# Cross-attention units of four heads by 256 tokens, and one time axis for all steps of the attention plan

## The reference

```python
x = x + attn(layernorm(x))          # 16 heads of 16; blocks of 128 tokens, each sees itself (causal) and the block before
x = x + xattn(layernorm(x), ctx, mask)   # 16 heads of 16; 77 context tokens, mask by token and context position
x = x + ffn(layernorm(x))           # gate/up 256 -> 704, silu(gate) * up, down; 8-bit fake quantisation of x, weights and h
```

## Time and profile before

| | before |
|---|---|
| median of 3 runs | 944.12 us (940.3 to 950.16) |
| the profiled execution | 945.94 us |
| its span, first to last instruction | 944.2 us |
| mean granted clock of TensorE | 0.866 |
| PE / DVE / ACT / POOL busy | 77% / 58% / 44% / 20% of the span |
| setup until the first score unit | 0 to 72 us |
| attention phases | 72 to 788 us |
| last chain to `out`, then the FFN | 788 to 944 us |

### The profile page before, as it was taken

The page is one execution under the profiler, slowest core; times in us unless marked ns, Lnnn a source line. Parts: engine busy times, 40 slices in busy tenths (PEclk is TensorE's granted clock), DMA queues, the critical chain, the costliest instruction groups (busy, mean ns, idle before and its releaser), DMA issues.

```text
span 944.2 us, 13998 instructions
## 1 busy us (share of the span) xinstructions
PE 728.0 (77%) x5008; PEld 412.4 (44%) x5008; DVE 544.3 (58%) x970; ACT 418.8 (44%) x610; POOL 192.4 (20%) x231
## 2 busy tenths in 40 slices
PE   3769888888788997989788778689795684468755
PEld 2446455555545443556445443435343221323344
DVE  4378546665854457566465753345652730559977
ACT  3414544434443544643343455132351342169865
POOL 4002121211321202110231031002002000334536
PEclk9968988899998999999898989688797565679979
DMA  8540141504221344151215413130344012000013
GB/s 258 181 134 3 51 134 42 141 14 115 70 82 30 94 104 109 48 150 48 63 47 134 98 41 86 37 108 14 86 108 130 14 40 45 0 1 1 1 45 134
DMA packets 59187, 71.78 MB, mean 76 GB/s; under 512 B 24635, under 2 KB 36079, under 8 KB 59119
## 3 DMA queue, kind: packets, MB, share of 16 engines
q1 hardware_dynamic: 43792, 50.90, 16.8%
q10 hardware_dynamic: 15327, 19.99, 10.6%
HBM read 17.74 MB, written 4.72 MB: 24 GB/s over the span
## 4 chain that ended last, share of the span: by engine, by line
PE 23%; DVE 12%; issue 6%; DMA 6%; ACT 4%; ACTq 4%; POOL 0%; SPq 0%; POOLq 0%; DVEq 0%
PE banks L676 6%; DMA oc<-sums 4%; PE banks L666 4%; ACTq L906 3%; PE banks L623 2%; PE banks L625 2%; PE banks L549 2%; DVE tops L1280 1%; PE banks L720 1%; PE banks L594 1%; DMA sums<-ls 1%; ACT big L882 1%; PE banks L596 1%; PE banks L653 1%; DVE big L1274 1%
## 5 line engine op out<-in xcount | busy, mean ns | idle before, releaser
L1109 DVE TENSOR_REDUCE mneg<-banks 128x4 f32<-128x1024 f32 (+1 forms) x128 | 145.7, 1152 | 73.8 <-PE banks L587 73.2
L1370 POOL TENSOR_SCALAR_AFFINE_SELECT big<-big 128x512 f32<-128x512 f32 x128 | 85.1, 665 | 448.3 <-ACT big L878 446.9
L878 ACT ACTIVATE big<-banks 128x1024 f32<-128x1024 f32 (+1 forms) x128 | 124.1, 973 | 107.1 <-PE banks L616 74.4
L584 PE MATMUL banks<-big 96*128 96x256 bf16 (+1 forms) x512 | 101.6, 296 | 22.2 <-DVE mneg L1109 9.1
L882 ACT ACTIVATE big<-banks 77x1024 f32<-77x1024 f32 x64 | 64.8, 1019 | 110.7 <-PE banks L625 84.6
L549 PE MATMUL banks<-xnT,weights 128*128 128x512 f32 x192 | 91.7, 607 | 3.0 <-DVE big L1082 1.2
L653 PE MATMUL banks<-big 128*17 128x256 f32 (+1 forms) x1152 | 80.1, 371 | 16.8 <-POOL big L1370 16.7
L1113 DVE TENSOR_REDUCE mneg<-banks 128x8 f32<-128x616 f32 x64 | 49.7, 793 | 68.9 <-PE banks L596 68.7
L616 PE MATMUL banks<-big 99*128 99x256 bf16 (+1 forms) x512 | 76.4, 273 | 9.7 <-ACT big L878 5.6
L587 PE MATMUL banks<-causal,identb 128*128 128x256 bf16 x256 | 77.6, 305 | 0.0
L584 PEld LDWEIGHTS banks<-big 96*128 96x128 bf16 x512 | 51.0, 109 | 58.8 <-issue 28.9
(11 more groups left out here) (150 smaller groups left out, 1165.2 us busy)
## 6 DMA issues: line engine op xcount, KB each, us to landing
big<-parts SPq DMA_DIRECT2D x288, 128.0 KB, 2.5
oc<-sums ACTq DMA_DIRECT2D x16, 512.0 KB
oTs<-oe ACTq DMA_DIRECT2D x64, 64.0 KB, 2.7
out_dram<-oTs SPq DMA_DIRECT2D x16, 256.0 KB, 2.1
xs<-in_x_dram SPq DMA_DIRECT2D x3, 1024.0 KB, 10.1
big<-oe ACTq DMA_DIRECT2D x32, 64.0 KB, 2.9
oTx<-oe ACTq DMA_DIRECT2D x32, 64.0 KB, 2.6
big<-kparts SPq DMA_DIRECT2D x96, 9.6 KB, 2.6
```

Of the source, the lines that this page charges most:

```text
L584: e.matmul(bank(p, j)[:, i * 256 + lo * 128:i * 256 + 256], Q[0:96, hh, c * 128:c * 128 + 128], K[0:96, hh, (c - 1 + lo) * 128:(c + 1) * 1 ...
L878: e.activation(pt[u].rearrange("p (i n) -> p i n", i=4)[:, :, 0:n], pair(p).rearrange("p j (s n) -> p (j s) n", s=2)[:, :, 0:n], ACT.Exp, ...
L1109: e.tensor_reduce(M.rearrange("p (h c) -> p h c", h=4)[:, :, c], pair(p).rearrange("p j (s n) -> p (j s) n", s=2)[:, :, lo * 128:256], AX. ...
L1370: e.affine_select(out=P[:, :, 0:128], in_=P[:, :, 0:128], compare_op=ALU.is_ge, fill=0.0, base=0, pattern=[[0, 4], [1, 128]], channel_mult ...
```

## The change

**Cross units.** Unit j of a cross phase is now tokens 256 j to 256 j + 255 of all four heads. A score unit is two banks (z); each gets two score matmuls of 256 columns and one mask matmul of 512 columns that reads the 256 mask columns twice. A val unit is four matmuls of 256 columns, one in each quarter of the array's columns; the bank of `acc` is still `j // 2`, and its halves are filled in turn.

**One time axis.** `PHASE_US` gives a self phase a length of 20 and a cross phase one of 11. `put` adds each step at `start + t * length`, `start` running over the phases, and all steps of all phases are sorted once and handed to the planner in one go. So a time below 0 or above 1 now reaches into the neighbouring phase. The last two vals of a phase are at 0.01 and 0.065 of the next one, behind its `score` 0 (at 0). The max steps of the next phase run from 0.04 (before -0.3) to 0.62, and those of a self job that follows a cross job from -0.75. `rows` is the last of these. Other times are moved by a few hundredths, the forced `proj` group has a time of its own (0.98), and followers are counted in steps as before.

```diff
--- before.py
+++ after.py
@@ -28,6 +28,7 @@
 AT = {j: n for n, j in enumerate(JOBS)}
 UNITS = {"s": NC, "x": 4}
 HALF_AT = {"s": 3, "x": 1}
+PHASE_US = {"s": 20.0, "x": 11.0}
 
 
 
@@ -157,42 +158,48 @@
     fw = weight_steps()
     fw_at = {28: (0, 1), 29: (1, 9), 30: (9, 15), 31: (15, 20)}
     tail, normed = [], {("s", 0)}
+    timed, start = [], 0.0
+
+    def put(steps):
+        timed.extend(((start + t * length, len(timed) + i, step) for i, (t, step) in enumerate(steps)))
+
     for p in range(2 * len(JOBS)):
         n, g = divmod(p, 2)
         job, units = JOBS[n], UNITS[JOBS[n][0]]
-        steps = [(-1, ("force", "rows"))] + over(-0.5, -0.1, tail)
+        length = PHASE_US[job[0]]
+        put([(-0.001, ("force", "rows"))] + over(0.01, 0.12, tail))
         for j in range(units):
-            steps.append((j / units, ("score", job, g, j)))
+            put([(j / units, ("score", job, g, j))])
             if j > 1:
-                steps.append((j / units + 0.001, ("val", job, g, j - 2, False)))
+                put([(j / units + 0.002, ("val", job, g, j - 2, False))])
         tail = [("val", job, g, units - 2, False), ("val", job, g, units - 1, True)]
         if p + 1 < 2 * len(JOBS):
-            steps += over(-0.3, 0.62, max_steps(p + 1))
+            early = job[0] == "x" and g == 1 and JOBS[n + 1][0] == "s"
+            put(over(-0.75 if early else 0.04, 0.62, max_steps(p + 1)))
         last = JOBS[n - 1] if n else ("s", 0, 0)
         if g == 0:
             if n + 1 < len(JOBS):
-                steps += over(0.05, 0.1, [("bulk", JOBS[n + 1], 1, z) for z in range(2)])
+                put(over(0.13, 0.18, [("bulk", JOBS[n + 1], 1, z) for z in range(2)]))
                 if JOBS[n + 1][0] == "s":
-                    steps += over(0.1, 0.5, [("v", JOBS[n + 1], c0) for c0 in (0, 4)]) if n else []
+                    put(over(0.14, 0.5, [("v", JOBS[n + 1], c0) for c0 in (0, 4)]))
                 else:
-                    steps += [(0.1, ("xkeys", JOBS[n + 1])), (0.15, ("bulk", JOBS[n + 1], 0, 1))]
-            if n == 0:
-                steps += over(0.05, 0.3, [("v", JOBS[1], c0) for c0 in (0, 4)])
+                    put([(0.14, ("xkeys", JOBS[n + 1])), (0.19, ("bulk", JOBS[n + 1], 0, 1))])
             if last[2] == 1 and (job[0] == "s" or last[0] == "x"):
-                steps += over(0.7 if job[0] == "s" else 0.9, 1.0, out_steps(*last[0:2]))
+                put(over(0.7 if job[0] == "s" else 0.85, 0.99, out_steps(*last[0:2])))
             if n + 2 < len(JOBS) and JOBS[n + 2][0:2] not in normed:
-                steps += over(0.0, 0.45, stats_steps(*JOBS[n + 2][0:2]))
+                put(over(0.0, 0.45, stats_steps(*JOBS[n + 2][0:2])))
                 normed.add(JOBS[n + 2][0:2])
         else:
             if last == ("s", last[1], 1) and job[0] == "x":
-                steps += over(0.1, 0.8, out_steps(*last[0:2]))
+                put(over(0.1, 0.8, out_steps(*last[0:2])))
             if n + 2 < len(JOBS):
-                steps += over(0.08, 0.7, [("force", "norm")] + qk_steps(JOBS[n + 2]))
+                put(over(0.1, 0.7, [("force", "norm")] + qk_steps(JOBS[n + 2])) + [(0.98, ("force", "proj"))])
             if last == ("x", last[1], 1):
-                steps += over(0.05, 1.0, third_steps(last[1]))
+                put(over(0.05, 0.97, third_steps(last[1])))
         if p in fw_at:
-            steps += over(0.2, 1.0, fw[slice(*fw_at[p])])
-        o.run([s for _, s in sorted(steps, key=lambda it: it[0])] + ([("force", "proj")] if g else []))
+            put(over(0.2, 0.97, fw[slice(*fw_at[p])]))
+        start += length
+    o.run([s for _, _, s in sorted(timed, key=lambda it: it[0:2])])
     o.run(tail)
     o.run([("force", "acc"), ("force", "weights")])
     a, z = out_steps("x", NB - 1), last_third_steps(NB - 1)
@@ -617,13 +624,14 @@
                                          ks[r][0:99, i, j * 128:j * 128 + 128], qs[r][0:99, i, j * 128:j * 128 + n],
                                          start=(i % 2 == 0), stop=True, skip_group_check=True)
                     else:
-                        blk, two = j // 2, j % 2
-                        for i in range(2):
-                            hh = 2 * two + i
-                            e.matmul(bank(p, i)[0:KX, :], xks[r][0:99, hh, :], qs[r][0:99, hh, blk * 512:blk * 512 + 512],
-                                     start=True, stop=False)
-                            t = e.matmul(bank(p, i)[0:KX, :], identb[0:KX, 0:KX], maskt[0:KX, blk * 512:blk * 512 + 512],
-                                         start=False, stop=True)
+                        keep = maskt[0:KX, j * 256:j * 256 + 256].rearrange("p (a n) -> p a n", a=1)
+                        for z in range(2):
+                            for i in range(2):
+                                e.matmul(bank(p, z)[0:KX, i * 256:i * 256 + 256], xks[r][0:99, 2 * z + i, :],
+                                         qs[r][0:99, 2 * z + i, j * 256:j * 256 + 256], start=(i == 0), stop=False,
+                                         skip_group_check=True)
+                            t = e.matmul(bank(p, z)[0:KX, :].rearrange("p (i n) -> p i n", i=2), identb[0:KX, 0:KX],
+                                         keep.to_broadcast([KX, 2, 256]), start=False, stop=True, skip_group_check=True)
                     t.then_inc(t_score, 1)
                 elif k == "val":
                     _, job, g, j, end = s
@@ -654,17 +662,16 @@
                                              va[f][:, j, 4 * g + i, :], P[:, i, a:z], start=new,
                                              stop=(j == 7 or z - a == 128), tile_position=(0, 32 * i), skip_group_check=True)
                     else:
-                        blk, two = j // 2, j % 2
                         if j == 0 and g == 0:
                             e.wait_ge(d_xv, 2 * n_of["xkeys", job])
                             e.wait_ge(p_one, 2 * n_of["xkeys", job])
                         if j == 2:
                             e.wait_ge(a_evac, before)
                         e.wait_ge(a_exp, n_of["score", job, g, j])
-                        for q in range(2):
-                            i = 2 * two + q
-                            t = e.matmul(acc[:, blk][32 * i:32 * i + 17, :], xv[r][0:KX, i, 0:17],
-                                         pt[u][0:KX, q * 512:q * 512 + 512], start=True, stop=True, tile_position=(0, 32 * i))
+                        for i in range(4):
+                            t = e.matmul(acc[:, j // 2][32 * i:32 * i + 17, (j % 2) * 256:(j % 2) * 256 + 256],
+                                         xv[r][0:KX, i, 0:17], pt[u][0:KX, i * 256:i * 256 + 256], start=(j % 2 == 0),
+                                         stop=True, tile_position=(0, 32 * i), skip_group_check=True)
                     t.then_inc(t_val, 1)
                 elif k == "out":
                     _, kind, b, c = s
```

## The result

| | before | changed |
|---|---|---|
| median, lowest and highest of four runs, us | 944.14 (940.3 to 950.16) | 989.98 (987.35 to 995.17) |
| ratio to before, with its 95% interval | | 1.0486 (1.0416 to 1.0556) |
| span of the profiled execution, us | 944.2 | 989.0 |
| mean granted clock | 0.866 | 0.85 |
| end of the last `val`, us | 787.7 | 833.0 |

The kernel is 45.8 us slower. The forecast was 972 us with a range of 928 to 998. In the kernel after, `max` is L591 and L601, `turnm` L611, `score` L623 and L630, `val` L661 and L672, `out` L683, `scale` L1153, the select L1377, and the DMA of the maxima is issued at L875.

What follows compares the result with a forecast made beforehand. PE's own work was taken to set the pace until 600 us, then chains of waits with PE at half speed. Terms -18 + 9 + 32 - 8 + 8 + 5 = +28 gave 972 us for the median, range 928 to 998.

Steps and rivals of the forecast that it cites:

- term 3: At phase boundaries, score 0 moved ahead of the tail waits for the row maxima to land: +32 us, bounds 0 and +45.
- Term 1: Cross units of four heads by 256: cheaper value matmuls, scores unchanged, -18 us, nearly all on PE's path.
- Term 2: At 31 phase boundaries, more changes between kinds of matmul, two more pieces each at 0.22 us: +9 us.
- Term 4: Max units no longer bunched, so fewer waits for banks VectorE or an exponential still holds: -8 us, bounds 0 and 17.
- Term 5: Chains from the last val to the output projection start later, behind score 0 and a max or two: +8 us.
- Term 6: New waits of 2 to 4 us at boundaries make PE's clock fall, three losses of 1.7 us: +5, bounds 0 and +25.
- The rival that priced fifteen falls at 1.7: The clock falls at nearly every boundary, fifteen new falls instead of three: +20, 992 us; chance 0.14.
- The faster rival: Maxima have landed when PE reaches score 0, so tail waits go and none replace them: -26, 918 us; chance 0.17.
- the draw: Waits for the maxima swallow other waits, +12 instead of +32, and the clock costs nothing: -1, 943 us; chance 0.17.

Runs made afterwards that it cites:

- e1: Kernel before with only the change's new cross units (four heads by 256), in the old order of steps: 938.48 us, ratio 0.9955.
- e10: e1, but from the third job on the maxima's DMA goes to DRAM and score 0 does not wait for it: 932.74 us, ratio 0.9873.
- e9: Changed kernel, but from the third job on the maxima's DMA goes to DRAM and score 0 does not wait for it: 940.06 us, ratio 0.9952.
- e6: Changed kernel with the last two vals of a phase side by side behind score 0: 981.25 us, ratio 1.0376.
- e8: e1 with two maxes moved ahead, one before and one between the last two vals: 944.24 us, ratio 0.9997.
- e12: e1 with turnm one step later behind rows (four steps instead of three): 941.14 us, ratio 0.9944.
- e2: Changed kernel with the old cross units (two heads by 512) put back, new order kept: 1022.99 us, ratio 1.0856.
- e3: Changed kernel with the first score unit of a phase behind the two last vals and a max or two: 963.77 us, ratio 1.0228.
- e7: Changed kernel with turnm one step behind rows instead of three: 974.21 us, ratio 1.0308.

## Why the prediction was right, and where it was short

The main step, term 3, was right in its mechanism and near its size. The sum fell 18 us short, 15 of them by the clock. Term by term:

- **Term 1, -18.** The saving came, but not as time. PE's busy time, work and clock's loss together, is 20.1 us less in e1; 12.5 came back as idle time, and the time fell by 4 us. The prediction took the saving as nearly all on PE's path: this was wrong. Of the -18 some 5 us are half clock (1.7 us instead of 0.8 in six phases), so in the table's columns the term is -13 of work, measured -12.9, and -5 of clock. The unit itself costs what it said: 0.55 us from 715.60 to 716.15, where it had said 0.56.
- **Term 2, +9.** 4.9 us of work between e1 and the changed kernel, 5.4 between e10 and e9, so it was about twice too large. The trace has the `val`s in 139 pieces in the old order and in 191 in the new one, 52 more and not 62; a piece costs 0.09 to 0.11 us by these pairs and by e6, where 0.22 was taken. In e8, which splits the `max`es more too, it is 0.16. Terms 1 and 2 together were -4 in work, and measured -8.0.
- **Term 3, +32.** Idle time at score 0 rose by 46.6 us and that before `val` fell by 16.8: +29.8. Without the very first wait, which lies ahead of the 72 us, it is +26.0. The latency was right too: the wait ended 2.96 to 4.17 us behind the DMA's issue, 3.1 in the median of the 23, for 3.3; and 3.94 us behind `turnm` at the boundary shown, for 3.7. The Trainium skill's fixed cost of about 2.0 us (DMA: Bandwidth & Descriptors, Anatomy of one DMA) would have made this term some 20 lower; the rows here show 2.8 us as the shortest. e9 and e10 show the cause by itself.
- **Term 4, -8.** Did not come. `max` and the other scores idle 39.1 us, 37.5 before, and 8.0 of the latter was the key transfer, which has no row now. Their waits for VectorE and ScalarE rose from 31 to 36 us, and those without a named releaser from 2.7 to 5.1. L591 waits 13.6 us for VectorE (9.1 before, whole span). Maxes one at a time between other units still find VectorE behind.
- **Term 5, +8.** The waits before `out` rose by 10.3 us, near the term's size, though no run separates the reason it gave; the key transfer, which I had among the six, has no row any more. The longest in the phases, from the view of the chain that ended last and PE's timeline, for the earlier trace rows:

```profile
756.23 1.57 DMA sums<-ls
...
757.82 7.02 DMA oc<-sums
```

```profile
766.23 1.19 PE L683 MATMUL banks<-weights,big 128*128 128x256 f32 x2 [8.14 <-DVE oTx L1153]
```

- **Term 6, +5.** This is the term that was mis-sized: +19.9, the upper part of its bounds. I counted three new falls of the clock at 1.7 us each. Between 72 us and the last `val` the trace's record of the granted clock has 19 stretches at half clock before and 22 after, so three more; that the number fits is partly luck, since e1 and e10, without the new waits, have 21 and 22. But in all these stretches last 236 us after and 188 before, and most of those behind 600 us last 10 us or more. The price of a fall was wrong. By the same steps in each kernel, that is the first 22 phases and the ten from X1b's first score unit on, again in us and in one execution of each:

| kernel | clock's loss, first 22 | clock's loss, last ten | idle, first 22 | idle, last ten |
|---|---|---|---|---|
| before | 34.0 | 35.7 | 72.4 | 46.5 |
| changed | 37.3 | 52.7 | 91.0 | 61.6 |
| e9 new order, no landing wait | 26.9 | 44.4 | 69.8 | 52.2 |
| e10 old order, no landing wait | 36.9 | 31.4 | 73.9 | 50.2 |

The last ten phases as stretches, before and then changed:

```profile
579.80:787.70 207.90, 161.40 (x855) 76.82 (x853) 96.16 (x217) 71.25 (x112) 15.52 (x17) 0.76 0.27 68
```

```profile
599.20:833.00 233.80, 172.18 (x1128) 97.60 (x1129) 96.58 (x217) 72.64 (x113) 15.69 (x19) 0.70 0.24 61
```

So 17.0 us of the loss came in the last ten phases, where the clock was down already, and 3.3 in the others. (e1 and e12, nearly the same kernel, differ by 7.1 in the first 22 and by 0.8 in the last ten.) e9 takes the landing waits away, and 10.4 us go in the first 22 phases and 8.3 in the last ten. There it keeps 44.4, 13.0 more than e10 without a single wait for a landing: the waits are about half of the new loss there, and what makes the other half is not shown. e8, in the old order and with the landing hidden, has 47.0 there too. The rival that priced fifteen falls at 1.7, 25 us of clock and 992 us in all, came nearer to the time than my sum did, but by luck: the falls did not become many, they became long. The Trainium skill (TensorE: Matmul & The Clock Gate, HAM oscillation) says that waits which recur in every tile let the clock fall each time. The trace agrees only in part: fifteen landing waits of 28 us behind the very first score unit, all in the first 22 phases, left the mean at 0.92, while the last ten, with seven of 20 us, had 0.70.

Idle time in all was forecast as 32 - 8 + 8 = +32 and measured as +33.5. That agreement is in part luck: term 3 was 6 us too large and the waits of `turnm` fell by 3.7, while the 8 us that term 4 took off did not come and term 5 was 2 too small. The faster rival (the maxima land in time) is refuted by the two rows of landing waits, the draw by e9: only 12 of 42.7 us of waits were swallowed by others. The 989.98 us measured are the upper edge of the 955 to 990 that the forecast covered. The interaction that e2 shows, old units losing their overlap when taken apart, I did not see; apart, the two halves give -4 and +80 us, both at once +46.

What stays open: what takes the clock down in the last ten phases, where its loss is 44 to 50 us in e3 to e9 and 30 to 31 in e1, e10 and e12; no kernel removed the waits there one by one. That a version much faster than both exists is not shown: e12 and e1 are below the kernel before by half a per cent, e10 by 1.3%, with other maxima subtracted than the rows' own.

## What to carry to other kernels

On an engine that runs in order, ask of each step that is moved ahead what it waits for and how much ready work stood between it and that event; a latency of 4 us from PE's transpose through ScalarE and a DMA back to PE is hidden or paid there, and moving its middle step moved most of the wait to another place (25.6 of 33.9 us in e7). Price the clock by stretch, not by a mean over the kernel, and compare stretches that hold the same steps. Waits cost clock besides their own time: 0.6 us for every idle one in the change and in its undoing (19.9 to 33.5, and 19.0 to 30.6 in e9), though this is no fixed price: e6 gave back 5.6 us of clock for 3.1 of idle time, and in e1 the clock's loss fell by 7.2 while the idle time rose by 12.5. And cost a saving in the places where its engine is late by its own work; inside a chain of waits it comes back as idle time.

## What the runs showed of the hardware

A DMA of 24 KB between two places in SBUF took 2.83 to 3.92 us from the start of its issue to its landing in the 23 cases that stand in the changed kernel's chain, the issue itself some 0.83 us of ScalarE's queue. The one case in the chain of the kernel before took 5.82 us, the longest of e7 5.68. Three rows from the chain that ended last, in the changed kernel:

```profile
92.03 2.83 DMA big<-m3t
...
141.67 3.92 DMA big<-m3t
...
718.46 3.06 DMA big<-m3t
```

Float32 units of two column tiles gain from their neighbours (0.97 us alone, 2.09 for three in a row); taken apart, the same 64 units took 62.6 us instead of 49.9 at full clock, and units of four tiles with half the columns 36.7 in the same order. Two kernels with the same work and idle time to 0.5 us (e1 and e12) had 62.6 and 70.7 us of clock loss in their profiled executions, so a difference of 8 us in that term needs more than one execution.
